# Fewer constant products at three seams, and the first recurrent item inside the convolution

## The reference, cut to what matters

```python
# L1: graph convolution, batch norm, hidden width 256, relu, back to 128, batch norm
agg = einsum('nm,bmd->bnd', A_hat, features)
h   = relu(batchnorm(agg @ W1.T + b1)); out = batchnorm(h @ W2.T + b2)
# L2: two graph convolutions, then windows of 1, 2, 3, 4 nodes through an LSTM
h = relu(einsum('ts,bsh->bth', adj, x @ Wg0 + bg0))
h = relu(einsum('ts,bsh->bth', adj, h @ Wg1 + bg1))
for p in range(1, MAX_SKIP + 1):
    wins = h[:, :nw * p, :].reshape(Bv * nw, p, Hd)
    last = _lstm_last(Wih[p-1], Whh[p-1], bih[p-1], bhh[p-1], wins)
    h = h.at[:, arange(nw) * p + (p - 1), :].set(last)
# one LSTM step: g = x_t @ Wih.T + h @ Whh.T + bias; i, f, gg, o = split(g)
# c = sigmoid(f) * c + sigmoid(i) * tanh(gg); h = sigmoid(o) * tanh(c)
```

## Time and profile before

| | us |
|---|---|
| median of three runs | 1219.66 |
| range | 1219.46 to 1221.11 |
| the profiled execution | 1221.55 |
| its span on the core | 1219.6 |
| PE busy | 1190.1 (98%) |
| DVE busy | 980.9 (80%) |
| ACT busy | 901.8 (74%) |
| POOL busy | 429.1 (35%) |

### The profile page before, as it was taken

One profiled execution on the slowest core, in us unless ns is written; L12 is line 12 of the kernel. 1 busy time (PEld: TensorE's weight loads), 2 busy tenths in 40 slices (PEclk: granted clock), 3 DMA queues, 4 the chain that ended last, 5 costly groups with the idle time before them and its releaser, 6 DMA issues.

```text
span 1219.6 us, 22497 instructions
## 1 busy us (share of the span) xinstructions
PE 1190.1 (98%) x7322; PEld 1034.3 (85%) x7322; DVE 980.9 (80%) x2009; ACT 901.8 (74%) x1733; POOL 429.1 (35%) x795
## 2 busy tenths in 40 slices
PE   9999999999999998999999999999999999989998
PEld 8999988874788886789878988898898899978997
DVE  5888859978688876888788878887887899988774
ACT  5766769968588876887787778776777688875554
POOL 5878748800267420000000000000000377757764
PEclk9999999999999998999999999999999999999999
DMA  8000000000311100000000000000300020001112
GB/s 322 2 1 2 1 1 1 0 1 0 113 64 66 69 35 1 1 1 1 1 1 1 1 1 1 1 1 1 138 1 1 15 125 1 2 1 52 70 71 86
DMA packets 14924, 38.23 MB, mean 31 GB/s; under 512 B 1904, under 2 KB 3952, under 8 KB 13808
## 3 DMA queue, kind: packets, MB, share of 16 engines
q1 hardware_dynamic: 14000, 36.60, 7.8%
q10 hardware_dynamic: 832, 0.46, 0.2%
HBM read 20.27 MB, written 16.78 MB: 30 GB/s over the span
## 4 chain that ended last, share of the span: by engine, by line
PE 75%; DVE 6%; ACT 4%; issue 1%; POOL 1%; POOLq 0%; DVEq 0%; ACTq 0%
PE psum L973 7%; PE psum L1219 7%; PE psum L1218 7%; PE psum L1220 7%; PE psum L1237 5%; PE psum L1233 4%; PE psum L1234 4%; PE psum L80 3%; PE psum L1506 2%; PE psum L1758 2%; PE psum L772 2%; PE psum L774 2%; PE psum L1723 2%; PE psum L1512 2%; PE psum L996 2%; PE psum L1733 2%
## 5 line engine op out<-in xcount | busy, mean ns | idle before, releaser
L1255 ACT ACTIVATE gates<-psum,lstm_bias 128x512 f32<-128x512 f32 (+1 forms) x504 | 302.4, 637 | 101.9 <-PE psum L1237 88.1
L153 POOL TENSOR_TENSOR l2r_sum<-l2r_st 128x8 f32<-128x8 f32 x16 | 5.2, 322 | 517.9 <-DVE l2r_st L126 517.6
L185 ACT ACTIVATE l_h<-X,nmr,rstd 128x128 f32<-128x128 f32 (+1 forms) x392 | 160.6, 484 | 14.2 <-POOLq L179 14.0
L1219 PE MATMUL psum<-lstm_node_hi,Wih_lo 128*128 128x512 f32 (+1 forms) x408 | 148.2, 363 | 0.0
L1220 PE MATMUL psum<-lstm_node_lo,Wih_hi 128*128 128x512 f32 (+1 forms) x408 | 148.0, 363 | 0.0
L1218 PE MATMUL psum<-lstm_node_hi,Wih_hi 128*128 128x512 f32 (+1 forms) x408 | 148.0, 363 | 0.0
L1233 PE MATMUL psum<-lstm_hid_hi,Whh_hi 128*128 128x512 f32 (+1 forms) x288 | 104.8, 364 | 3.9 <-DVE lstm_hid_hi L1314 3.8
L1237 PE MATMUL psum<-lstm_hid_lo,Whh_hi 128*128 128x512 f32 (+1 forms) x288 | 108.0, 375 | 0.0
L1234 PE MATMUL psum<-lstm_hid_hi,Whh_lo 128*128 128x512 f32 (+1 forms) x288 | 103.5, 359 | 0.0
L1260 ACT ACTIVATE gates<-lstm_cell 128x512 f32<-128x512 f32 (+1 forms) x144 | 83.7, 581 | 21.0 <-DVE lstm_cell L1301 20.6
L1218 PEld LDWEIGHTS psum<-lstm_node_hi,Wih_hi 128*128 128x128 f32 x408 | 77.2, 189 | 10.8 <-ACT gates L1255 0.3
(11 more groups left out here) (277 smaller groups left out, 3476.0 us busy)
## 6 DMA issues: line engine op xcount, KB each, us to landing
x_spill<-X SPq DMA_DIRECT2D x32, 256.0 KB, 2.0
X<-x_spill SPq DMA_DIRECT2D x2, 4096.0 KB, 13.0
out<-X SPq DMA_DIRECT2D x32, 256.0 KB, 2.0
X<-in_x SPq DMA_DIRECT2D x6, 1024.0 KB, 16.7
X<-in_x SPq DMA_DIRECT2D x3, 512.0 KB, 8.6
w_raw<-in_WihT SPq DMA_DIRECT2D x1, 1024.0 KB, 5.4
w_raw<-in_WhhT SPq DMA_DIRECT2D x1, 1024.0 KB, 9.1
X<-in_x SPq DMA_DIRECT2D x2, 256.0 KB, 3.3
```

Of the source, the lines that this page charges most:

```text
L185: last = act.activation(h[:, j, :], k.X[:, bass.ds(b0, TB), :][:, j, :], ACT.Relu, bias=k.nmr[:, bass.ds(b0, TB)][:, j:j + 1], scale=k.rst ...
L1219: pe.matmul(out, lo, x_high, start=False, stop=False)
L1255: act.activation(gate_of(it, g), k.bank[4 * s + g][:, 0:it.N], ACT.Tanh if g == GATE_G else ACT.Sigmoid, bias=k.lstm_bias[:, it.p - 1, g:g ...
```

## The change

Five things change.

1. At the seams fewer constant products are issued: ahead of stage_gcn_out 18 instead of 44 (12 of the stage before stay in front of them), behind it 9 instead of 12, ahead of stage_conv's steps 12 instead of 22, and in its first steps 3, 4, 18, 1 instead of 6, 6, 30, 2.
2. The input products of item a0 (nine products) are issued by TensorE in the convolution, ahead of step 34, and its three gates by ScalarE at the same place.
3. The inputs of a0, a1, b0 and b1 are split by GpSimd, behind its last coefficients of the convolution, instead of by ScalarE and VectorE.
4. PSUM banks of stage_conv are renumbered so that a0's banks are free: the pipeline's four products go to banks 4 to 7, the constant products to bank 3. The gate of slot 1 that shares bank 7 waits for the last H at its first use.
5. Buffers move in SBUF: `shift` uses the place of `W2T`, and room is kept for the early inputs; one counting semaphore is shared by two stages.

The core of the diff:

```diff
-        stay_awake(pe, k, k.bank[7], 44)
+        stay_awake(pe, k, k.bank[7], 18)
...
-        stay_awake(pe, k, k.bank[7], 12)
+        stay_awake(pe, k, k.bank[7], 9)
...
-    FILL = {-2: 6, -1: 6, 0: 30, 1: 2}
+    FILL = {-2: 3, -1: 4, 0: 18, 1: 1}
...
-    psZ, psG, psV2, psH, psS = k.bank[2:7]
+    psZ, psG, psV2, psH = k.bank[4:8]
+    psS, unread = k.bank[2:4]
...
-    def steps(eng, step):
+    def steps(eng, step, between={}):
...
+                t = (2 * j + c // S) * S + c % S
+                if isinstance(t, int) and t in between:
+                    between[t](eng)
...
-        stay_awake(pe, k, k.bank[7], 22)
-        steps(pe, step)
+        stay_awake(pe, k, unread, 12)
+        steps(pe, step, between)
...
+    ON_POOL = 2
+    due = {n - LEAD: it for n, it in enumerate(items) if it.p == 1 and it.tile >= ON_POOL}
-    at_once = [it for it in items[:LEAD] if it.p == 1]
...
+    def x_halves_at_start(pool, it):
+        s = it.slot
+        hi, lo = x_halves(it)
+        zeros = k.zero[:, 0:1].unsqueeze(2).broadcast_to([P, it.nw, it.nb])
+        pool.tensor_tensor(out=hi, in0=node_of(it), in1=zeros, op=ALU.add).then_inc(xh_ready[s], 1)
+        pool.wait_ge(xh_ready[s], it.tile + 1)
+        pool.tensor_tensor(out=lo, in0=node_of(it), in1=hi.bitcast(F32), op=ALU.subtract).then_inc(xl_ready[s], 1)
...
     def on_pool(pool):
+        pool.wait_ge(conv.H_done, GROUP // TB + ON_POOL)
+        for it in tiles:
+            if it.tile < ON_POOL:
+                x_halves_at_start(pool, it)
...
+            elif s == 1 and g == GATE_O:
+                pe.wait_ge(conv.H_done, conv.tiles)
...
+    def first_products(pe):
+        pe.wait_ge(*conv.w_split)
+        input_products(pe, items[0])
...
+    def first_gates(act):
+        for g in items[0].gates:
+            gate(act, items[0], g)
...
+    last_step = conv.tiles + 2
+    programs.early_tensor, programs.early_scalar, programs.early_vector = {last_step: first_products}, {last_step: first_gates}, {}
```

More of the change, by code:

```diff
@@ L967, in on_scalar, with on_tensor @@
         act.wait_ge(bn_ready, 1)
-        steps(act, step)
-    def on_tensor(pe):
+        steps(act, step, between)
+    def on_tensor(pe, between):
         def product(ps, lhs, rhs, done):
@@ L1126, in stage_lstm_to_attend @@
     sb = lambda n, t=F32: each(S, lambda s: ctx.enter_context(nc.sbuf_tensor(f"lstm_{n}{s}", [P, TW], t)))
-    gates = each(S, lambda s: ctx.enter_context(nc.sbuf_tensor(f"gates{s}", [P, 4, TW], F32)))
+    gate_tiles = lambda s: ctx.enter_context(nc.sbuf_tensor(f"gates{s}", [P, 4, TW], F32))
+    second = gate_tiles(1)
+    hid_hi, hid_lo = (sb(n, F32R) for n in ("hid_hi", "hid_lo"))
+    gates = [gate_tiles(0), second]
     cell = sb("cell")
-    hid_hi, hid_lo = (sb(n, F32R) for n in ("hid_hi", "hid_lo"))
     x_hi, x_lo = (each(2, lambda b: sb(f"{n}{b}", F32R)) for n in ("x_hi", "x_lo"))
@@ L1196, in on_pool, with passes, input_products @@
         sc.on_pool(pool, at)
         at.on_pool(pool)
+    def passes(it, W, g):
+        return [W[n][:, it.p - 1, g * P:(g + 1) * P] for n in range(2)]
+    def input_products(pe, it):
+        s = it.slot
+        if it.p == 1:
+            x_high, x_low = x_halves(it)
+            pe.wait_ge(xl_ready[s], it.tile + 1)
+        else:
+            x_high, x_low = node_halves(it)
+            pe.wait_ge(lo_ready[s], it.source)
+        for g in it.gates:
+            if it.emptied[g]:
+                pe.wait_ge(act_out[s], it.emptied[g])
+            elif s == 1 and g == GATE_O:
+                pe.wait_ge(conv.H_done, conv.tiles)
+            out = columns(it, k.bank[4 * s + g])
+            hi, lo = passes(it, k.Wih, g)
+            pe.matmul(out, hi, x_high, start=True, stop=False)
+            pe.matmul(out, lo, x_high, start=False, stop=False)
+            last = pe.matmul(out, hi, x_low, start=False, stop=it.step == 0)
+            if it.step == 0:
+                last.then_inc(done[s], 1)
@@ L1199, in on_tensor @@
+    def first_products(pe):
+        pe.wait_ge(*conv.w_split)
+        input_products(pe, items[0])
     def on_tensor(pe):
-        def passes(it, W, g):
-            return [W[n][:, it.p - 1, g * P:(g + 1) * P] for n in range(2)]
-        pe.wait_ge(*conv.w_split)
         for it in items:
             s = it.slot
[L1207 to L1222, removed]
+            if it is not items[0]:
+                input_products(pe, it)
@@ L1263, in x_high @@
             s = it.slot
-            if it.tile >= 2:
-                two_back = next(o for o in tiles if o.slot == s and o.tile == it.tile - 2)
-                act.wait_ge(done[s], gate_count(two_back, GATE_O))
+            two_back = next(o for o in tiles if o.slot == s and o.tile == it.tile - 2)
+            act.wait_ge(done[s], gate_count(two_back, GATE_O))
+            act.wait_ge(xl_ready[s], ON_POOL)
             act.activation(x_halves(it)[0], node_of(it), ACT.Copy).then_inc(xh_ready[s], 1)
-        for it in at_once:
-            x_high(it)
         before = None
@@ L1275, in on_scalar @@
                 before = None
-            for g in it.gates:
+            for g in it.gates if n else ():
                 if g == GATE_O and before:
                     tanh_of_cell(before)
-                gate(it, g)
+                gate(act, it, g)
             if n in due:
@@ L1960, in _ @@
                 gcn_out.on_scalar(act)
-                conv.on_scalar(act)
+                conv.on_scalar(act, states.early_scalar)
                 states.on_scalar(act)
@@ L1967, in _ @@
                 gcn_out.on_tensor(pe)
-                conv.on_tensor(pe)
+                conv.on_tensor(pe, states.early_tensor)
                 states.on_tensor(pe)
```

54 lines of the change are left out of this document (27 added, 27 removed).

## The result

| | before, us | after, us |
|---|---|---|
| median | 1219.46 (5 runs) | 1206.99 (5 runs) |
| range | 1218.03 to 1221.11 | 1206.69 to 1208.82 |
| the profiled execution | 1221.55 | 1208.81 |
| its span | 1219.6 | 1207.0 |

The ratio is 0.9904, with a 95% interval of 0.989 to 0.9918: the changed kernel is 1% faster, about 12 us. Four more runs beside later experiments gave 1206.55, 1208.31, 1208.32 and 1208.41. So the nine runs fall into two levels, four at 1206.55 to 1206.99 and five at 1208.31 to 1208.82, and their median is 1208.31.

The account below looks back on a forecast made before the run. TensorE, busy 98% of the span, was taken as the bound, with constant products on its chain. The terms -3.0 + 1.7 - 4.2 - 5.7 = -11.2 us took the median from 1219.66 to 1208.5 us; 8-in-10 range 1205.0 to 1212.0.

Parts of the forecast that it names:

- the rival with the held clock: Into stage_gcn_out: TensorE's idle does not lower the clock, so -12.9 us in all, 1206.8 us; chance 0.2.
- seam A, start of L772: Into stage_gcn_out: with fewer constant products the first real product waits for VectorE's `O_stored` and starts sooner, -3.0 us.
- seam A, clock: Into stage_gcn_out: 2.6 us of TensorE idle most likely lowers the clock, +1.7 us, bounds 0 and 3.4.
- seam B: Into stage_conv: fewer constant products let transposes, first normalised tile and V2 start sooner, -4.2 us, bounds -2.65 and -4.9.
- seam C: Into the recurrence: a0's products behind V2 and GpSimd's input splits bring b0's cell sooner, -5.7 us, bounds -3.0 and -7.4.
- fall at the first second steps: At 496.1 us, the recurrence's second steps: low clock taken as staying; its absence, 1.7 us, only in the bound.
- One fall more: At stage_conv's start or the recurrence's head: another low-clock stretch from idle gaps, +1.7 us, 1210.2 us; chance 0.2.
- The slower case: Through stage_gcn_out: the clock falls and stays down, up to 1234.3 us; chance 0.03.

## Why the prediction was right

The forecast for the profiled execution was 1210.35, and it took 1208.81. The forecast for the median was 1208.5: the five runs of the comparison have 1206.99, 1.5 below it and beside the rival with the held clock (1206.8); all nine have 1208.31. Where a median of these runs lands depends on how many of them hold a fall of the clock, so the nearness of 1208.31 is in part luck. What was right is the mechanism at each seam:

| step | predicted | measured |
|---|---|---|
| seam A, start of L772 | -3.0 | -3.22 from the first constant product on (-3.2 in four other profiles) |
| seam A, clock | +1.7 | +1.7 where it falls: in both profiles, in at most 5 of 9 runs by their level |
| seam B | -4.2 | -4.11 |
| seam C | -5.7 | -5.78, of which 1.89 clock |
| fall at the first second steps | 0, bound 1.7 | gone in the profile: -1.56 |

**Seam A.** The wait that took the place of the constant products was the one named, `O_stored`, 2.41 us long where 2.6 was said, and the experiments on its place confirm it: moved, L772 starts at 256.0. The start came 0.2 sooner than forecast, 0.14 of it because the flag does not wait for the end of the copy (257.93 now), which the prediction took as its time. The clock's price was of the right size, but the sum took it as given, from one idle stretch each of 2.02 and 1.79 us, with 0.2 left for the other case. It is an event of some executions.

The Trainium skill (TensorE: Matmul & The Clock Gate, section Why this matters for your kernels) warns only against longer idle gaps than these; by that rule the clock holds at seam A. Two profiles of the changed kernel disagree, with 2.41 and 2.39 us of idle before 3.4 us at 0.50; the profile of the kernel with b1 split by the other engines agrees, with 2.40 us and a full clock.

**Seam B.** The sum was right, its parts less so. The transposes start 2.44 sooner relative to the seam's start (319.89 - 314.52 against 323.48 - 315.67), not 2.65: 0.16 of the difference is that the chain's 315.83 was set against ScalarE's times from the timeline. The first normalised product starts 4.4 sooner, not 4.9. That product waits 0.83 instead of 1.0, and V2's first 0.67 instead of 1.4. These waits lie inside the 4.11; the relu at 334.61 against 339.85 is 4.1 sooner relative to the seam's start, as worked out, and it is what sets V2.

**Seam C.** Each instant followed: the nine products at 0.23 each at full clock; H 3.08 behind V2's start where 3.04 was worked out (464.1 - 461.06); the G gate 5.24 sooner (forecast 5.2), b0's cell 5.76 (forecast 5.7). GpSimd's work cost nothing. What the prediction did not see is that 1.89 us of this were a low stretch that the kernel before has in some executions only.

**The sum.** The four pieces of the profiled execution are -1.15 (seam A up to the next seam's start, with its clock, and with the stage ahead 0.28 later), -4.11, -5.78 and -1.56, together -12.6 of the 12.74 measured; the rest lies outside the span. The forecast of -11.2 misses the last piece: the fall at 496.1, which the idle of 1.78 us at the same place did not bring this time. From the first second-step product to the end of the span the kernels take 724.38 us before and 722.82 after; over all profiles it is 722.2 to 722.8 without that fall and 724.2 to 724.4 with it.

That the forecast of -11.2 equals what the work alone gives (3.2 + 4.1 + 3.9) is luck: the 1.7 charged at seam A and the 1.89 of clock inside seam C's 5.7 nearly cancel. The first is paid in some executions, the second was held by some of the old ones.

**Levels.** So the times of single runs are a sum of work and of falls: 1.7 us at seam A, 1.9 at the old recurrence's start, 1.5 at the second steps, 0.4 at the attention's start (722.24 in the one profile without it, 722.6 to 722.8 in seven that have it). Lowest runs come nearest to the work alone: 1217.80 before, 1213.99 with the new recurrence alone (3.8 less; its order gave 3.9), 1210.38 with the new counts alone (7.4 less; 3.2 + 4.1 = 7.3), 1206.55 with both (11.25 less; 3.9 + 7.3 = 11.2). That the levels are the clock shows in the mean granted clock on record with each run: in the 27 runs of the kernel before beside the experiments it is 0.998 or 0.999 at 1217.80 to 1218.38, 0.996 or 0.997 at 1219.01 to 1219.63, and 0.994 or 0.995 at 1220.33 to 1221.85. In which place a fall was only the profiles show; for a run without one it is inferred from the sizes.

**The rivals.** "The clock holds at seam A" (1206.8, chance 0.2) is, as far as the levels tell, the lower level of the same kernel, four runs of nine at 1206.55 to 1206.99, and the median of the comparison with them: not another case, but the other half of this one. "One fall more" occurred in none of its two profiles, and no run reached its 1210.2. The slower case is excluded: behind the fall the clock is full again after 3.4 us.

## What to carry to other kernels

When constant products are taken away ahead of a seam, look for the flag that is raised late on another engine behind work that could wait: here it held 1.5 us that were had by moving two lines up. Keep enough of them that the idle time behind them is short; 0.88 us was free, 2.4 cost 1.7 us in four profiles of five. Where runs lie at levels 1.5 to 2 us apart, compare the lowest runs, the granted clock of each and the distances within profiles, not medians alone: a median of five can carry a fall or not.

## What the runs showed of the hardware

An idle stretch of the same length at the same place lowers TensorE's clock in one execution and not in another. At seam A 2.39 to 2.41 us did in four profiles (twice the changed kernel, the new counts alone, a0 one step later) and 2.40 did not in a fifth. At the old recurrence's start 2.02 us did in one profile and not in another. Ahead of the second steps 1.77 to 1.79 us did in five profiles and not in seven. At the attention's start 2.33 or 2.34 us did in twelve profiles, and 2.34 us in the thirteenth, with b1 split elsewhere, did not. A gap of 1.32 to 1.34 us shortly ahead of it did in none of the thirteen, nor did 0.88 and 0.21 us at seam A in the three profiles that have them. What decides between two executions is not settled here.

The longer idle stretch was not the dearer one here: in one profile, the 6.42 us without any constant product brought 6.8 us at 0.50, half of it inside the idle time, and cost the work behind it 1.7 us, as 2.41 us did.
